# A three-stage decoder layer on one core: other orders, PSUM banks and waits in the third stage

## The chip, the core and the metric

The kernel runs on one core of a Trainium2 chip. The core's engines are TensorE (PE in the profile; its weight loads are a row of their own, PEld), VectorE (DVE), ScalarE (ACT), GpSimd (POOL) and SyncE (SP, which only issues transfers). Each works through its own instructions in order; they meet through semaphores. The metric is the device time of one execution in microseconds (us), as the median of several.

## The reference, cut to what matters

`x` is 64 sequences of 64 tokens, 128 wide. A self attention and a cross attention come first. The third part, which is where the change lies, is six layers of local attention and a gated feed-forward, each on the shifted residual:

```python
for i in range(DEPTH):                      # 6
    x = attn_layer(shift_tokens(x), Wqkv[i], q_scale[i], k_scale[i], Wo[i]) + x
    x = ffn_layer(shift_tokens(x), ln_g[i], ln_b[i], W1[i], b1[i], W2[i], b2[i]) + x

# attn_layer, 16 heads of 64:
q, k, v = heads(x @ Wqkv)
q = l2norm(q) * qs;  k = l2norm(k) * ksc
q = q * cos * scale + rotate_half(q) * sin * scale
k = k * cos * inv + rotate_half(k) * sin * inv
out = softmax(8 * q k^T, masked) v
return out @ Wo

# ffn_layer, inner width 341:
a, gate = split(layernorm(x) * g + bln) @ W1 + b1
return a * gelu(gate) @ W2 + b2
```

## The kernel before

A tile is two sequences, 128 tokens, so a layer has 32 tiles and the third stage (the function `local`) has N = 192 of them. It is one software pipeline: every engine runs a loop over `i`, and each body names the steps of an iteration with the tile that each works on, for instance `queries(i, 0)` beside `scores(i - 1)`, `head_outputs(i - 4)` and `ff_in(i - 7)`. In a full iteration TensorE thus does one of each step, for tiles of different age. Nothing schedules this: the order in an engine's loop is the order in which it works, and the waits are written by hand.

The steps, by their lines in the profile, in TensorE's order before: the turned input (L1008, `bank<-ident,ystat`), the output projection (L1160), the four products that make queries and keys (L1032), the turning of queries and keys (L1008, `bank<-ident,R`), the second feed-forward product (L1024), the turning of the probabilities (L1008, `bank<-ident,P`) and of the normalised input (L1008, `bank<-ident,xn`), the **value products** `head_outputs` (probabilities times values, L1144, 32 products of 64x64), the **scores** (mask L1098, then L1103, 32 products of 64x64), the **values** (L1083, 4 products of 512 columns), and the first feed-forward product (L1128). A float32 product is two MATMUL records and two LDWEIGHTS records in the trace, so 32 products read as x64.

ScalarE copies each result out of PSUM (L1194: `xcT`, `qT`, `kT`, `PT`, `OT`, `V`), squares queries and keys (L1219), and takes exponents (L1232) and gates (L1259). VectorE makes the rotation (L1319), the sums of squares (L1332), maxima, row sums and the gated product. GpSimd issues two accumulating transfers per tile, `queries_added` (L1419) and `keys_added` (L1424), which add the rotated half to the other in place in `R`; it refines the inverse lengths in twelve small operations (L1465 to L1472), scales keys (L1432) and scores (L1438), and makes the probability products (`probs_scaled`, L1444, `P<-P,inv_sum`).

PSUM has eight banks and every step uses a fixed one. A bank that two steps share makes the later wait for whoever reads the earlier result; most waits at the head of TensorE's steps are of that kind. A `Counted` semaphore counts several parts per tile, and its list says in which order they come, so a changed order changes these lists too.

## Time and profile before

| | |
|---|---|
| time, median of 3 runs | 3522.41 us (3520.82 to 3523.2) |
| time of the profiled execution | 3525.89 us, its span 3524.1 us |
| TensorE clock granted, mean | 0.993 of full speed |
| TensorE matmul busy | 3377.9 us, 96% of the span |
| VectorE, ScalarE, GpSimd busy | 80%, 79%, 70% |
| third stage, first input turned | at 569.4 us, the last at 3446.0 us |

The span runs from the first to the last instruction. Busy time is when an instruction of that engine is recorded; a float32 product's second record overlaps the first, and a record's end is modelled, so that a busy share of 96% is not a measure of what is lost between products. In the chain of work the pieces follow each other without overlap; in the timeline they overlap.

### The profile page before, as it was taken

Reading aid. Unit: us, or ns where it says so; the run is one execution under the profiler, and the core shown is the slowest. Engines: PE = TensorE matmul, PEld = TensorE weight load, DVE = VectorE, ACT = ScalarE, POOL = GpSimd, SP = SyncE. Lnnn points to the kernel's source line nnn. Section 1 sums busy time; section 2 is a strip of 40 time slices with the busy share of each in tenths; the row PEclk is TensorE's granted clock in tenths of the full one; section 3 lists DMA queues with packets and bytes.
Section 4 is the critical chain, followed back from the end, with each engine's and each line's share of the span. In section 5 each row is a group of like instructions: output and inputs, shape, how many; then the busy total and the mean of one; then the engine's idle time right before and its main releaser. Section 6 shows DMA issues by size and latency. Waiting matters only on the chain.

```text
span 3524.1 us, 120975 instructions
## 1 busy us (share of the span) xinstructions
PE 3377.9 (96%) x49605; PEld 2495.3 (71%) x49605; DVE 2811.5 (80%) x5297; ACT 2792.7 (79%) x5522; POOL 2475.5 (70%) x4812
## 2 busy tenths in 40 slices
PE   8989997999999999999999999999999999999997
PEld 5778774677777777777777777777777777777776
DVE  6834445888888888888888888888888888888885
ACT  5756664688888888888888888888888888888885
POOL 5622224777777777777777777777777777777774
PEclk9999998999999999999999999999999999999999
DMA  3000002444444444444444444444444444444441
GB/s 101 3 10 8 9 6 50 92 82 82 82 81 89 95 82 82 80 88 97 82 82 82 83 90 93 82 82 80 90 96 83 82 82 88 78 85 83 88 85 39
DMA packets 200382, 260.17 MB, mean 74 GB/s; under 512 B 123161, under 2 KB 145438, under 8 KB 199838
## 3 DMA queue, kind: packets, MB, share of 16 engines
q0 software_dynamic: 55296, 201.35, 30.4%
q1 hardware_dynamic: 143820, 50.88, 5.8%
q8 instruction: 400, 6.55, 0.8%
q14 instruction: 144, 1.18, 0.1%
q10 hardware_dynamic: 722, 0.21, 0.0%
HBM read 23.95 MB, written 2.10 MB: 7 GB/s over the span
## 4 chain that ended last, share of the span: by engine, by line
PE 78%; issue 2%; DVE 1%; POOL 1%; DMA 1%; ACT 0%; SPq 0%; POOLq 0%; DVEq 0%
PE bank L1032 18%; PE bank L1008 16%; PE bank L1083 10%; PE bank L1160 10%; PE bank L1128 7%; PE bank L1144 6%; PE bank L1103 5%; PE bank L1024 3%; PE bank L1098 2%; DVE R L1319 1%; DMA R<-R 1%; POOL R L1432 0%; POOL P L1444 0%; DVE ss L1332 0%; POOL P L1438 0%
## 5 line engine op out<-in xcount | busy, mean ns | idle before, releaser
L1319 DVE TENSOR_TENSOR R<-bank,tables 128x1024 f32<-128x1024 f32 x768 | 903.6, 1218 | 167.5 <-ACT sq L1219 127.4
L1032 PE MATMUL bank<-WA,xcT 128*128 128x512 f32 x1536 | 757.6, 596 | 1.8 <-ACT xcT L1194 1.8
L1008 PEld LDWEIGHTS bank<-ident,R 128*128 128x128 f32 x3072 | 371.6, 141 | 307.0 <-issue 299.9
L1444 POOL TENSOR_TENSOR P<-P,inv_sum 128x512 f32<-128x512 f32 x384 | 458.2, 1193 | 13.1 <-DVE inv_sum L1373 12.1
L1332 DVE TENSOR_REDUCE ss<-sq 128x16 f32<-128x1024 f32 x384 | 460.3, 1199 | 0.0
L1219 ACT ACTIVATE sq<-bank 128x512 f32<-128x512 f32 x768 | 438.2, 595 | 23.9 <-PE bank L1032 23.5
L1432 POOL TENSOR_TENSOR R<-R,rn 128x512 f32<-128x512 f32 x384 | 392.3, 1042 | 88.1 <-DMA R<-R 73.4
L1008 PE MATMUL bank<-ident,R 128*128 128x128 f32 x3072 | 429.8, 273 | 3.3 <-POOL R L1432 2.4
L1438 POOL TENSOR_TENSOR P<-P,rn 128x512 f32<-128x512 f32 x384 | 402.5, 1048 | 2.1 <-DVE P L1361 2.1
L1160 PE MATMUL bank<-WO,OT 128*128 128x128 f32 x3072 | 386.4, 279 | 1.7 <-ACT OT L1194 1.7
L1083 PE MATMUL bank<-WV,xcT 128*64 128x512 f32 x1536 | 376.0, 606 | 3.2 <-DVE R L1319 2.9
L1160 PEld LDWEIGHTS bank<-WO,OT 128*128 128x128 f32 x3072 | 357.4, 192 | 5.3 <-ACT OT L1194 1.9
L1194 ACT ACTIVATE PT<-bank 128x512 f32<-128x512 f32 x384 | 230.2, 599 | 146.8 <-PE bank L1008 146.8
L1194 ACT ACTIVATE kT<-bank 128x512 f32<-128x512 f32 x384 | 233.3, 608 | 133.6 <-PE bank L1008 133.6
L1032 PEld LDWEIGHTS bank<-WA,xcT 128*128 128x128 f32 x1536 | 248.6, 192 | 97.2 <-issue 94.3
L1128 PE MATMUL bank<-xnT,W 128*128 128x128 f32 (+1 forms) x2304 | 287.5, 275 | 0.0
L1194 ACT ACTIVATE V<-bank 128x512 f32<-128x512 f32 x384 | 230.5, 600 | 71.9 <-PE bank L1083 71.9
L1008 PEld LDWEIGHTS bank<-ident,P 128*128 128x128 f32 x1536 | 170.8, 141 | 164.1 <-issue 155.1
L1103 PE MATMUL bank<-kT,qT 64*64 64x64 f32 x12288 | 234.5, 219 | 54.6 <-issue 54.6
L1103 PEld LDWEIGHTS bank<-kT,qT 64*64 64x64 f32 x12288 | 229.7, 135 | 71.0 <-issue 61.9
L1361 DVE TENSOR_TENSOR P<-bank,mx 128x512 f32<-128x512 f32 x384 | 263.2, 686 | 6.7
L1128 PEld LDWEIGHTS bank<-xnT,W 128*128 128x128 f32 (+1 forms) x2304 | 264.8, 180 | 0.1
(154 smaller groups left out, 7082.5 us busy)
## 6 DMA issues: line engine op xcount, KB each, us to landing
R<-R POOLq DMA_DIRECT2D x384, 512.0 KB, 5.3
WA<-in_wqkv SPq DMA_DIRECT2D x24, 256.0 KB, 2.8
ystat<-Y SPq DMA_DIRECT2D x192, 32.0 KB
ystat<-Y SPq DMA_DIRECT2D x384, 15.8 KB
ys<-Y SPq DMA_DIRECT2D x192, 32.0 KB
ys<-Y SPq DMA_DIRECT2D x384, 15.8 KB
WV<-in_wqkv SPq DMA_DIRECT2D x6, 512.0 KB, 5.9
WO<-in_wo SPq DMA_DIRECT2D x6, 512.0 KB, 4.3
```

The lines of the kernel that those rows point to most:

```text
L1008: return nc.tensor.transpose(dst, src, m.ident[:, :])
L1032: mm(b[QK_BANK[n, half]][:, :], m.xsT[:, t % 2, :], cols[:, half, :, :], start=True, stop=True)\
L1083: last = mm(V_BANK[bb][64 * e:64 * e + 64, :], m.xsT[:, t % 2, bb * 64:bb * 64 + 64], cols[:, e, :, :], start=True, stop=True)
L1103: last = mm(S_BANK[a][64 * bb:64 * bb + 64, hp * 64:(hp + 1) * 64], m.qT[head, t % 2, at:at + 64], m.kT[head, t % 2, at:at + 64], start=Fa ...
L1128: last = mm(FF_BANK[c][0:rows, side * 128:(side + 1) * 128], m.W1[:, off + at:off + at + rows], m.xnT[:, t % 2, :], start=True, stop=True)
L1160: last = mm(OUT[:, 0:128], m.OT[:, t % 2, at:at + 128], wo[:, c * 128:(c + 1) * 128], start=(c == 0), stop=(c == PAIRS - 1))
L1194: return nc.scalar.activation(dst, src, ACT.Copy)
L1219: nc.scalar.activation(by_half[:, half, :, :], b[QK_BANK[n, half]][:, :].rearrange("p (h d) -> p h d", d=32), ACT.Square)\
L1319: tt(both, src.unsqueeze(1).to_broadcast([128, 2, 16, 32]), tab.unsqueeze(2).to_broadcast([128, 2, 16, 32]), ALU.mult).then_inc(s.rotated. ...
L1332: nc.vector.tensor_reduce(m.ss[:, t % 2, 16 * n:16 * n + 16], m.sq[:, n, :].rearrange("p (h d) -> p h d", d=HD), AX.X, ALU.add)\
L1438: tt(part, part, wide(m.rn[:, t % 4, a:16:2]), ALU.mult).then_inc(s.scaled.sem, 1)
L1444: tt(part, part, wide(m.inv_sum[:, t % 2, 8 * a:8 * a + 8]), ALU.mult).then_inc(s.normal.sem, 1)
```

## The change

It writes the loops of TensorE, ScalarE, VectorE and GpSimd in the third stage in another order, gives every step other PSUM banks, and writes the waits that the new sharing needs. No instruction is added or removed: there are as many products, copies, reductions and transfers, of the same shapes. GpSimd's `probs_scaled(i - 2, 1)` at an iteration's end becomes `probs_scaled(i - 3, 1)` behind the next one's `queries_added`, and `inverse_deviation` moves from the end of one iteration to behind `keys_added` of the next. The core of the diff:

```diff
-    QK_BANK = {(QUERIES, 0): 3, (QUERIES, 1): 6, (KEYS, 0): 1, (KEYS, 1): 2}
-    TURNED_IN, TURNED_OUT = b[4], b[6]
-    KT_BANK, QT_BANK, V_BANK = (b[7], b[0]), (b[7], b[4]), (b[1], b[4])
-    S_BANK, PT_BANK, PV_BANK = (b[5], b[6]), (b[0], b[0]), (b[4], b[3])
-    OUT, FF_BANK, FF_OUT = b[0], (b[2], b[1], b[7]), b[5]
+    QK_BANK = {(QUERIES, 0): 6, (QUERIES, 1): 5, (KEYS, 0): 7, (KEYS, 1): 1}
+    TURNED_IN, TURNED_OUT = b[6], b[5]
+    KT_BANK, QT_BANK, V_BANK = (b[2], b[4]), (b[0], b[3]), (b[2], b[5])
+    S_BANK, PT_BANK, PV_BANK = (b[0], b[7]), (b[6], b[5]), (b[4], b[6])
+    OUT, FF_BANK, FF_OUT = b[4], (b[2], b[1], b[3]), b[3]
...
             def input_turned(t):
                 if exists(t):
                     pe.wait_ge(s.ystat[t % 2], 48 * (t // 2) + 48)
-                    at_least(pe, s.v_copied.sem, s.v_copied.upto(1, t))
+                    at_least(pe, s.p_copied.sem, s.p_copied.upto(0, t - 3))
                     turned(TURNED_IN[:, 0:128], m.ystat[:, t % 2, :]).then_inc(s.x_turned, 1)
...
             def keys_turned(t, j):
                 if exists(t):
                     pe.wait_ge(s.k_scaled.sem, s.k_scaled.upto(j, t + 1))
-                    if j == 0:
-                        pe.wait_ge(s.q_copied.sem, s.q_copied.upto(0, t + 1))
-                    elif t < 8:
-                        at_least(pe, s.y1, t - 3)
                     for n in range(4):
                         at = j * 512 + n * 128
                         last = turned(KT_BANK[j][:, n * 128:(n + 1) * 128], m.R[:, KEYS, 0, at:at + 128])
...
             def values(t, bb):
                 if exists(t):
                     cols = m.WV[:, :].rearrange("p (j e n) -> p e j n", e=2, n=128)
-                    if bb == 0:
-                        pe.wait_ge(s.rotated.sem, s.rotated.upto((KEYS, 0), t + 1))
+                    if bb == 1:
                         pe.wait_ge(m.w_v, 16 * layer(t) + 16)
+                        at_least(pe, s.xn_copied, t - 5)
+                        if t < 7:
+                            pe.wait_ge(s.rotated.sem, s.rotated.upto((QUERIES, 1), t + 1))
                     else:
-                        at_least(pe, s.o_copied.sem, s.o_copied.upto(0, t - 3))
+                        at_least(pe, s.k_copied.sem, s.k_copied.upto(0, t))
                     for e in range(2):
...
             def scores(t):
                 if exists(t):
-                    pe.wait_ge(s.q_copied.sem, s.q_copied.upto(1, t + 1))
+                    pe.wait_ge(s.q_copied.sem, s.q_copied.upto(0, t + 1))
                     pe.wait_ge(s.k_copied.sem, s.k_copied.upto(0, t + 1))
-                    at_least(pe, s.xn_copied, t - 4)
-                    at_least(pe, s.y, t - 6)
-                    if t < 6:
-                        pe.wait_ge(s.rotated.sem, s.rotated.upto((QUERIES, 1), t + 2))
+                    pe.wait_ge(s.rotated.sem, s.rotated.upto((KEYS, 0), min(t + 2, N)))
+                    if t == N - 1:
+                        pe.wait_ge(s.less.sem, s.less.upto(1, t))
...
                     pe.wait_ge(s.v_copied.sem, s.v_copied.upto(0, min(t + 8, N)))
-                    pe.wait_ge(s.rotated.sem, s.rotated.upto((KEYS, 1), min(t + 8, N)))
+                    at_least(pe, s.y, t)
+                    if t == 0:
+                        pe.wait_ge(s.rotated.sem, s.rotated.upto((KEYS, 1), 8))
...
                 input_turned(i)
                 out_projection(i - 5)
                 queries(i, 0)
-                queries_turned(i - 1, 1)
                 queries(i, 1)
                 queries_turned(i - 1, 0)
+                queries_turned(i - 1, 1)
                 keys(i, 0)
                 keys(i, 1)
                 keys_turned(i - 1, 1)
+                ff_out(i - 8)
                 keys_turned(i - 1, 0)
-                ff_out(i - 8)
-                probs_turned(i - 3, 1)
                 normal_turned(i - 6)
                 head_outputs(i - 4)
+                values(i, 1)
+                values(i, 0)
                 scores(i - 1)
-                values(i, 0)
-                values(i, 1)
+                probs_turned(i - 3, 1)
                 probs_turned(i - 3, 0)
                 ff_in(i - 7)
...
                 gates(i - 8)
                 squares(i, QUERIES, 0)
                 squares(i, QUERIES, 1)
+                queries_out(i - 1, 1)
                 queries_out(i - 1, 0)
+                keys_out(i - 1, 1)
+                squares(i, KEYS, 1)
+                normal_out(i - 6)
                 squares(i, KEYS, 0)
-                keys_out(i - 1, 1)
-                queries_out(i - 1, 1)
-                squares(i, KEYS, 1)
                 keys_out(i - 1, 0)
-                normal_out(i - 6)
+                values_out(i, 1)
+                exponents(i - 2, 1)
+                outputs_out(i - 4, 1)
+                outputs_out(i - 4, 0)
+                values_out(i, 0)
+                probs_out(i - 3, 1)
+                probs_out(i - 3, 0)
                 exponents(i - 2, 0)
-                outputs_out(i - 4, 0)
-                probs_out(i - 3, 1)
-                exponents(i - 2, 1)
                 normalised(i - 5)
-                outputs_out(i - 4, 1)
-                values_out(i, 0)
-                probs_out(i - 3, 0)
-                values_out(i, 1)
...
                 squares_summed(i, QUERIES)
-                ff_added(i - 8)
                 rotary(i, KEYS, 0)
                 rotary(i, KEYS, 1)
                 squares_summed(i, KEYS)
+                ff_added(i - 8)
                 seeded(i)
                 maximum(i - 1, 0)
-                maximum(i - 1, 1)
-                less_maximum(i - 1, 1)
                 row_sums(i - 2, 0)
                 less_maximum(i - 1, 0)
+                row_sums(i - 2, 1)
+                maximum(i - 1, 1)
+                attention_added(i - 4)
+                inverse_sums(i - 2, 1)
+                gated(i - 7)
+                less_maximum(i - 1, 1)
                 inverse_sums(i - 2, 0)
-                attention_added(i - 4)
-                gated(i - 7)
-                row_sums(i - 2, 1)
-                inverse_sums(i - 2, 1)
...
                 queries_added(i)
+                probs_scaled(i - 3, 1)
                 probs_scaled(i - 3, 0)
                 keys_added(i)
+                inverse_deviation(i - 5)
                 inverse_lengths(i)
+                keys_scaled(i, 1)
+                scores_scaled(i - 1, 0)
                 keys_scaled(i, 0)
-                keys_scaled(i, 1)
                 scores_scaled(i - 1, 1)
-                probs_scaled(i - 2, 1)
-                scores_scaled(i - 1, 0)
-                inverse_deviation(i - 4)
```

What stands in TensorE's row in the middle of a full iteration, before, from the second feed-forward product (L1024) to the first (L1128). `P` are the probabilities, `xn` the normalised input, `PT,V` the value products, `kT,qT` the scores, `WV,xcT` the values:

```order
L1024 MATMUL bank<-W,H 128x128 x3
L1008 MATMUL bank<-ident,P 128x128 x4
L1008 MATMUL bank<-ident,xn 128x128
L1144 MATMUL bank<-PT,V 64x64 x32
L1098 MATMUL bank<-causalb,identb 64x512 x4
L1103 MATMUL bank<-kT,qT 64x64 x32
L1083 MATMUL bank<-WV,xcT 64x512 x4
L1008 MATMUL bank<-ident,P 128x128 x4
L1128 MATMUL bank<-xnT,W 128x128 x4
```

The same piece of TensorE's row in the change:

```order
L1008 MATMUL bank<-ident,R 128x128 x4
L1025 MATMUL bank<-W,H 128x128 x3
L1008 MATMUL bank<-ident,R 128x128 x4
L1008 MATMUL bank<-ident,xn 128x128
L1146 MATMUL bank<-PT,V 64x64 x32
L1082 MATMUL bank<-WV,xcT 64x512 x4
L1096 MATMUL bank<-causalb,identb 64x512 x4
L1101 MATMUL bank<-kT,qT 64x64 x32
L1008 MATMUL bank<-ident,P 128x128 x8
L1130 MATMUL bank<-xnT,W 128x128 x4
```

Value products and scores stood side by side with only the mask's four products between them; now the four products of the values stand between the two. Both turnings of the probabilities stand behind the scores, where one stood ahead of the value products.

ScalarE's row before, from the exponents (`P<-P`) of an iteration's middle to the turned input's copy (`xcT`) of the next:

```order
L1194 ACTIVATE OT<-bank 128x512
L1194 ACTIVATE PT<-bank 128x512
L1232 ACTIVATE P<-P 128x512
L1242 ACTIVATE xn<-ys,nmr,rstd 128x128
L1194 ACTIVATE OT<-bank 128x512
L1194 ACTIVATE V<-bank 128x512
L1194 ACTIVATE PT<-bank 128x512
L1194 ACTIVATE V<-bank 128x512
L1194 ACTIVATE xcT<-bank 128x128
L1259 ACT_TABLE_LOAD
L1259 ACTIVATE G<-bank,b1col 128x128 x2
```

ScalarE's row in the change, from the copies of queries to the second exponents:

```order
L1193 ACTIVATE qT<-bank 128x512 x2
L1193 ACTIVATE kT<-bank 128x512
L1218 ACTIVATE sq<-bank 128x16x32
L1208 ACTIVATE xnT<-bank,bcol,gcol 128x128
L1218 ACTIVATE sq<-bank 128x16x32
L1193 ACTIVATE kT<-bank 128x512
L1193 ACTIVATE V<-bank 128x512
L1231 ACTIVATE P<-P 128x512
L1193 ACTIVATE OT<-bank 128x512 x2
L1193 ACTIVATE V<-bank 128x512
L1193 ACTIVATE PT<-bank 128x512 x2
L1231 ACTIVATE P<-P 128x512
```

The first copy of values (`V<-bank`) now stands ahead of exponents and outputs, and between the two copies of values stand one exponent and both copies of outputs. The fourth squares (`sq`) stand behind the copy of the normalised input.

GpSimd's row before, from the scaled keys (`R<-R,rn`) to the second accumulating transfer (`DMA R<-R`):

```order
L1432 TENSOR_TENSOR R<-R,rn 128x512 x2
L1438 TENSOR_TENSOR P<-P,rn 128x512
L1444 TENSOR_TENSOR P<-P,inv_sum 128x512
L1438 TENSOR_TENSOR P<-P,rn 128x512
L1450 TENSOR_SCALAR vare<-mv 128x1
L1452 TENSOR_TENSOR rstd<-vare,minus_half 128x1
L1454 TENSOR_SCALAR nmr<-mv,rstd 128x1
L1419 DMA R<-R 128x1024
L1444 TENSOR_TENSOR P<-P,inv_sum 128x512
L1424 DMA R<-R 128x1024
```

GpSimd's row in the change, from the first scaled keys to the inverse deviation:

```order
L1431 TENSOR_TENSOR R<-R,rn 128x512
L1437 TENSOR_TENSOR P<-P,rn 128x512
L1431 TENSOR_TENSOR R<-R,rn 128x512
L1437 TENSOR_TENSOR P<-P,rn 128x512
L1418 DMA R<-R 128x1024
L1443 TENSOR_TENSOR P<-P,inv_sum 128x512 x2
L1423 DMA R<-R 128x1024
L1449 TENSOR_SCALAR vare<-mv 128x1
L1451 TENSOR_TENSOR rstd<-vare,minus_half 128x1
L1453 TENSOR_SCALAR nmr<-mv,rstd 128x1
```

Both probability products (`P<-P,inv_sum`) stand between the two transfers' issues, where one stood, and the three small operations of the inverse deviation stand behind the second issue, ahead of the inverse lengths.

## Rows read from the trace of the kernel before

**Rows 1.** The page: busy time, share of the span and instructions of each engine

```profile
PE 3377.9 (96%) x49605; PEld 2495.3 (71%) x49605; DVE 2811.5 (80%) x5297; ACT 2792.7 (79%) x5522; POOL 2475.5 (70%) x4812
```

**Rows 2.** Tile `ystat`, 710 to 3447 us: duration min/median/max ns, first and last start us

```profile
L1008 PE MATMUL bank<-ident,ystat x182: 299/299/303, 710.0 to 3446.0; 128*128 128x128 f32 x182
```

**Rows 3.** The chain, an iteration without a stop: start us, us, what

```profile
1060.30 1.85 PE bank L1160 x16
...
1064.31 0.44 PE bank L1008 x4
...
1068.55 1.09 PE bank L1144 x64
1069.64 0.36 PE bank L1098 x4
1070.01 0.93 PE bank L1103 x64
1070.94 1.87 PE bank L1083 x8
1072.81 0.59 PE bank L1008 x4
1073.39 1.33 PE bank L1128 x12
...
1074.96 1.85 PE bank L1160 x16
```

**Rows 4.** The chain, the scores of two iterations with a stop

```profile
1053.98 0.69 PE bank L1103 x47
1054.67 1.14 issue
1055.82 0.47 PE bank L1103 x17
...
2143.26 0.31 PE bank L1103 x19
2143.57 1.05 issue
```

**Rows 5.** Waits, 710 to 3447 us, TensorE: us in total, times, longest

```profile
PE bank L1103 <- issue: 53.7, 59, 1.5
```

**Rows 6.** Transfer queues (packets, MB, share of 16 engines): whole span, then 1053.0 to 1053.4 us

```profile
q8 instruction: 400, 6.55, 0.8%
...
q8 instruction: 1, 0.02, 20.2%
```

**Rows 7.** Timeline: start us, us, engine, what, idle before and whom for

```profile
1070.71 0.65 ACT L1232 ACTIVATE P<-P 128x512 f32<-128x512 f32 x1
...
1071.61 0.61 ACT L1194 ACTIVATE OT<-bank 128x512 f32<-128x512 f32 x1
1072.09 0.62 ACT L1194 ACTIVATE V<-bank 128x512 f32<-128x512 f32 x1
...
2009.27 1.94 PE L1083 MATMUL bank<-WV,xcT 128*64 128x512 f32 x8
...
2010.39 0.60 ACT L1194 ACTIVATE V<-bank 128x512 f32<-128x512 f32 x1 [0.80 <-PE bank L1083]
```

**Rows 8.** Timeline, GpSimd and TensorE in the iteration of rows 3

```profile
1061.72 2.04 POOL L1432 TENSOR_TENSOR R<-R,rn 128x512 f32<-128x512 f32 x2 [0.98 <-DMA R<-R]
...
1066.30 1.04 PE L1008 MATMUL bank<-ident,R 128*128 128x128 f32 x8
...
1067.71 0.23 POOL L1450 TENSOR_SCALAR vare<-mv 128x1 f32<-128x1 f32 x1 [0.93 <-DVE mv L1327]
...
1068.90 0.94 POOL L1419 DMA_DIRECT2D R<-R  x1
...
1071.49 0.88 POOL L1424 DMA_DIRECT2D R<-R  x1 [0.56 <-DVE R L1319]
1073.05 0.23 POOL L1465 TENSOR_TENSOR rn_a<-seed 128x32 f32<-128x32 f32 x1 [0.69 <-DVE seed L1344]
```

More of the change, by code:

```diff
@@ L913, in local @@
     s.x_turned, s.x_copied = sem("local_x_turned"), sem("local_x_copied")
-    s.qk, s.squared, s.rotated = counted("qk", *four), counted("squared", *four), counted("rotated", *four)
+    s.qk, s.squared, s.rotated = counted("qk", *four), counted("squared", (QUERIES, 0), (QUERIES, 1), (KEYS, 1), (KEYS, 0)), counted("rotated", *four)
     s.summed, s.seed, s.lengths = counted("summed", QUERIES, KEYS), sem("local_seed"), sem("local_lengths")
-    s.q_added, s.k_added, s.k_scaled = sem("local_q_added"), sem("local_k_added"), counted("k_scaled", 0, 1)
+    s.q_added, s.k_added, s.k_scaled = sem("local_q_added"), sem("local_k_added"), counted("k_scaled", 1, 0)
     s.k_turned, s.k_copied = counted("k_turned", 1, 0), counted("k_copied", 1, 0)
-    s.q_turned, s.q_copied = counted("q_turned", 1, 0), counted("q_copied", 0, 1)
-    s.v, s.v_copied = counted("v", 0, 1), counted("v_copied", 0, 1)
-    s.scores, s.mx, s.less = sem("local_scores"), counted("mx", 0, 1), counted("less", 1, 0)
-    s.scaled, s.probs, s.row_sum = counted("scaled", 1, 0), counted("probs", 0, 1), counted("row_sum", 0, 1)
-    s.inverse, s.normal = counted("inverse", 0, 1), counted("normal", 1, 0)
+    s.q_turned, s.q_copied = counted("q_turned", 0, 1), counted("q_copied", 1, 0)
+    s.v, s.v_copied = counted("v", 1, 0), counted("v_copied", 1, 0)
+    s.scores, s.mx, s.less = sem("local_scores"), counted("mx", 0, 1), counted("less", 0, 1)
+    s.scaled, s.probs, s.row_sum = counted("scaled", 0, 1), counted("probs", 1, 0), counted("row_sum", 0, 1)
+    s.inverse, s.normal = counted("inverse", 1, 0), counted("normal", 1, 0)
     s.p_turned, s.p_copied = counted("p_turned", 1, 0), counted("p_copied", 1, 0)
-    s.o, s.o_copied, s.wo, s.y1 = sem("local_o"), counted("o_copied", 0, 1), sem("local_wo"), sem("local_y1")
+    s.o, s.o_copied, s.wo, s.y1 = sem("local_o"), counted("o_copied", 1, 0), sem("local_wo"), sem("local_y1")
     s.stats, s.var, s.vare, s.pow, s.rstd = (sem("local_stats"), sem("local_var"), sem("local_vare"), sem("local_pow"),
@@ L981, in weights @@
                     if 2 <= n < 6:
-                        at_least(sp, s.v.sem, s.v.upto(1, first))
+                        at_least(sp, s.v.sem, s.v.upto(0, first))
                         load_input_weights(sp, m, l + 1, (l + 1) % 2, n - 2)
@@ L990, in weights @@
                     if n == TILES - 1:
-                        sp.wait_ge(s.v.sem, s.v.upto(1, first + TILES))
+                        sp.wait_ge(s.v.sem, s.v.upto(0, first + TILES))
                         load_value_weights(sp, m, l + 1)
@@ L1039, in queries @@
                         pe.wait_ge(m.w_in, 64 * layer(t) + 64)
-                    else:
-                        at_least(pe, s.less.sem, s.less.upto(1, t - 1))
                     heads_in(t, QUERIES, half)
@@ L1045, in keys @@
                 if exists(t):
-                    if half == 1 and t < 2:
-                        at_least(pe, s.rotated.sem, s.rotated.upto((KEYS, 1), t))
+                    if half == 0:
+                        at_least(pe, s.less.sem, s.less.upto(1, t - 1))
+                    if t < 2:
+                        at_least(pe, s.rotated.sem, s.rotated.upto((KEYS, half), t))
                     heads_in(t, KEYS, half)
@@ L1065, in queries_turned @@
                     if j == 0:
+                        at_least(pe, s.less.sem, s.less.upto(0, t))
+                    else:
                         at_least(pe, s.h, 3 * (t - 6))
-                    elif t == N - 1:
-                        pe.wait_ge(s.v_copied.sem, s.v_copied.upto(1, t + 1))
                     for n in range(4):
@@ L1111, in probs_turned @@
                     if j == 0:
-                        pe.wait_ge(s.p_copied.sem, s.p_copied.upto(1, t + 1))
+                        at_least(pe, s.o_copied.sem, s.o_copied.upto(1, t))
                     else:
-                        pe.wait_ge(s.k_copied.sem, s.k_copied.upto(1, min(t + 3, N)))
+                        pe.wait_ge(s.v_copied.sem, s.v_copied.upto(1, min(t + 4, N)))
+                        if t >= N - 3:
+                            pe.wait_ge(s.xn_copied, t - 2)
                     for n in range(4):
@@ L1215, in squares @@
                     act.wait_ge(s.qk.sem, s.qk.upto((n, half), t + 1))
-                    if half == 0:
+                    if (n, half) in ((QUERIES, 0), (KEYS, 1)):
                         at_least(act, s.summed.sem, s.summed.upto(n, t))
@@ L1311, in rotary @@
                         if n == QUERIES:
-                            at_least(dve, s.q_turned.sem, s.q_turned.upto(0, t))
-                        elif t < 9:
+                            at_least(dve, s.q_turned.sem, s.q_turned.upto(1, t))
+                        elif t < 7:
                             at_least(dve, s.k_turned.sem, s.k_turned.upto(0, t))
@@ L1427, in keys_scaled @@
                 if exists(t):
-                    if j == 0:
+                    if j == 1:
                         pool.wait_ge(s.k_added, 16 * t + 16)
```

8 lines of the change are left out of this document (3 added, 5 removed).

## Prediction

> **What bounds the kernel now.** I read the page first: TensorE is busy for 96% of the span, the next engine for 80% [rows 1]. So the question is at what pace TensorE's row runs, and what interrupts it. For the pace I took the 182 turned inputs from the tenth iteration on: they start at 710.0 and, the last, at 3446.0 us, so 181 periods of 15.12 us [rows 2]. Then I followed the chain of work through single iterations. In the undisturbed one every piece is TensorE's and each begins where the one before ends; from output projection to output projection it takes 1074.96 - 1060.30 = 14.66 us [rows 3]. So the average iteration loses 15.12 - 14.66 = 0.46 us, over 181 of them 82.5 us. That is what a change without fewer instructions can win.
>
> The chain says where: in the scores. Undisturbed, their 64 records take 0.93 us [rows 3]. In other iterations the chain has 47 of them, then 1.14 us of "issue", then 17; or 19, then 1.05 us, then the rest [rows 4]. A wait for data would stand ahead of a step's first product, never behind the 47th or the 19th. The list of waits has 59 such stops in these 181 iterations, 53.7 us idle, the longest 1.5 us [rows 5]. Idle time is counted from the modelled end of the last product, so it understates: the first of the two shown makes the scores 0.69 + 1.14 + 0.47 = 2.30 us, 1.37 longer than undisturbed for 1.14 shown. With 0.23 us more for each of the 59, they cost 67 us of the 82.5. The next largest wait of a TensorE product in that stretch is under 2 us in total, so I put most of the remaining 15 us down to stops too short to show behind a modelled end.
>
> What is late is code. The queue of kind "instruction" moves 400 packets, 6.55 MB, 16.4 KB each [rows 6]; TensorE has 2 x 49605 records [rows 1], 248 to a packet. A packet begins within 1053.0 to 1053.4 us and takes 0.202 x 16 x 0.4 = 1.29 us [rows 6], so it lands between 1054.3 and 1054.7; the scores go on at 1055.82 [rows 4]. From its start to the resumption are 2.4 to 2.8 us. Value products, mask and scores are 128 + 8 + 128 = 264 records, more than a packet holds, and run through in 1.09 + 0.36 + 0.93 = 2.38 us [rows 3]; the other steps run at 0.11 us a product or slower [rows 3]. So only there can TensorE use up a portion before the next is in, and only where a portion ends in the scores does it show.
>
> **The change, part by part.** Nothing is added or removed, so the sum has only waits and joints.
>
> *Values between value products and scores.* The four value steps take 1.87 us [rows 3] and issue only 16 records. Where the portion was asked for during the value products, they put 1.87 us ahead of the same record of the scores; the longest stop was 1.5 us idle, some 1.7 lost [rows 5, 4]. So the stops that are due to this pair vanish. The bounds: nothing vanishes (0), or all that iterations lose (82.5 us). A portion that runs out behind the scores instead meets the turnings and the feed-forward product, which take 0.11 us a product [rows 3] and so leave time. I take 82.5 less 2 for some short stops that stay: **-80 us**.
>
> *Joints between steps of different shape.* Four turnings take 0.44 us behind a product of their own width and 0.59 us behind the values [rows 3], so a joint can cost 0.15 us. The values now stand between two steps in quarters of the array, and the probabilities' turnings leave the values' side. One joint more or fewer is at most 0.15 x 191 = 29 us either way; counting both orders, one is gained where one is lost, and I take 0.
>
> *ScalarE's copy of values, for which the first feed-forward product waits.* Its bank is now shared with the second half of the values. A copy starts 1.12 us after the values start [rows 7]. Behind it stand one exponent and two copies of outputs, a copy each 0.48 us after the last, the exponent at most 0.65, the copy itself 0.62 [rows 7]: 1.12 + 0.48 + 0.65 + 0.48 + 0.48 + 0.62 = 3.83 us after the values' start. TensorE arrives at the feed-forward product after 1.87 + 0.36 + 0.93 + 8 x 0.11 = 4.04 us. It is hidden by the scores and the turnings, with 0.2 us to spare; gone, each 0.1 us costs 19 us.
>
> *GpSimd: both probability products between the issues, the deviation behind the second.* Before, the second issue comes 2.59 us after the first and has idled 0.56 us for VectorE's rotation [rows 8]. The remaining 2.03 us are the issue, 0.94, and one product, 1.09. With two products it is 3.12 us, 0.5 too long, if the first issue stayed put. It doesn't: the deviation, 1.19 us from 1067.71 to 1068.90 [rows 8], and one product no longer stand ahead of it. Behind the second issue the deviation's 1.19 us now delays the inverse lengths, which used to idle 0.69 us for VectorE [rows 8]: at most 0.5 us later. The scaled keys start 1.42 us into the iteration (1061.72 - 1060.30), the first half is done 1.0 later, and TensorE wants it at 1066.30, 6.0 us in: 3.5 us of cover [rows 8]. Cost 0. The keys' rotation, whose squares now stand behind two more ScalarE steps of half a microsecond, comes out of the same cover.
>
> *VectorE* is busy for 80% [rows 1]; its maxima and row sums change places with 2.9 us an iteration to spare. Cost 0.
>
> Sum against the profiled execution: span 3524.1 - 80 = 3444 us. The median of the runs shown, 3522.4, is 1.7 lower: **3442 us**.
>
> **The rivals.**
>
> *Some stops stay.* GpSimd's first transfer is issued up to 2 us earlier, over the value products, and its packets then share the engines with the code's. If that makes portions late by half a microsecond more, the stops near the scores' end stay: a third of them, 27 us, gives 3469. For it: the packet's own time varies. Against: 1.87 us of cover for a mean loss of 67 / 59 = 1.1 us a stop.
>
> *A small new wait each iteration.* The 0.2 us at the feed-forward product are the thinnest cover I found. If ScalarE is 0.4 us later than laid out, TensorE waits 0.2 us, 191 x 0.2 = 38 us: 3480.
>
> *It doesn't do what I say.* The stops go to another place in the row, or have another cause: 3522. The Trainium skill, "Runtime: NRT & Kernel Launch", section "Instruction fetch mechanics", speaks for that: TensorE holds 2048 instructions and crossing a block is mostly hidden. By that rule the order of steps could not matter, and the time stays at 3522. The trace speaks against it: stops at changing places inside a step, and a packet that lands 1.1 to 1.5 us before the scores go on [rows 4, 6].
>
> *Slower.* GpSimd is one row, and the keys for TensorE stand behind two rotations, a transfer, twelve small operations and a product. If VectorE's keys come so late that this chain uses up its 3.5 us of cover, TensorE waits in every iteration; it decides from 3.5 + 0.46 = 4.0 us of lateness on. At 4.2 us the period is 14.66 + 0.7 = 15.36, and 191 x 0.24 = 46 us make 3568. I count at most 0.5 us from GpSimd and 1 us from ScalarE, so this needs a wait that I have not seen.
>
> **How the numbers follow.** Likeliest, 65 in 100: the stops go, 3442 us; its own range, from the joints and the uncounted 15 us, is 3426 to 3458. Some stops stay 13, a new small wait 9, no effect 8, slower 5. The range 3426 to 3482 holds the likeliest case in most of its spread and the next two for the most part, together about 8 in 10. A measurement of this kernel can tell about 0.2%, 7 us, from no change: faster 0.87, within it 0.07, slower 0.06.
>
> **What would show it right or wrong.** Right: the waits of TensorE on "issue" in the scores fall from 53.7 us to under 5, the mean period from 15.12 to 14.7, and 400 instruction packets stay. Wrong: "issue" at another line with a like sum; TensorE waiting for `V` at L1130, or for the scaled keys at L1008, some 190 times; a free iteration that is not 14.66 but 14.8 (joints).

## The result, and the profile after

The changed kernel takes 3399.44 us (median of 4, 3397.73 to 3402.21) against 3522.80 (3520.82 to 3524.92): a ratio of 0.965, with a 95% interval of 0.9634 to 0.9667, or 123 us less. The forecast was 3442, 80 us less; the measured time lies outside its range of 3426 to 3482, on the fast side.

The page after, engines and the queue of code [rows 1, 6], and the turned inputs from the tenth iteration on [rows 2]:

```profile
PE 3315.8 (98%) x49605; PEld 2471.6 (73%) x49605; DVE 2767.3 (81%) x5297; ACT 2803.6 (82%) x5522; POOL 2481.0 (73%) x4812
...
q8 instruction: 399, 6.54, 0.8%
```

```profile
L1008 PE MATMUL bank<-ident,ystat x182: 272/273/273, 704.6 to 3322.2; 128*128 128x128 f32 x182
```

Instructions and code are as many. The period is (3322.2 - 704.6) / 181 = 14.46 us, where it was 15.12 and 14.7 was forecast. One more number has changed without being looked for: the same turning is recorded with 273 ns instead of 299. The chain after, one iteration, to be held against [rows 3]:

```profile
1066.26 1.79 PE bank L1159 x16
...
1072.80 0.67 PE bank L1025 x6
1073.47 0.55 PE bank L1008 x5
1074.02 1.09 PE bank L1146 x64
1075.11 1.87 PE bank L1082 x8
1076.98 0.34 PE bank L1096 x4
1077.32 0.93 PE bank L1101 x64
1078.25 1.02 PE bank L1008 x8
1079.27 1.33 PE bank L1130 x12
1080.60 0.11 PE bank L1008
1080.71 1.34 PE bank L1159 x12
```

From output projection to output projection 1080.71 - 1066.26 = 14.45 us, 0.21 less than the undisturbed iteration of before. Value products, scores, values and the feed-forward product read the same. What is shorter is the output projection, 1.79 for 1.85, and what lies between the last feed-forward product and it. The list of waits, 710 to 3300 us, has no wait of a TensorE product at all in this kernel. GpSimd waits there (us in total, times, longest) for VectorE before the second issue, and hardly for a transfer:

```profile
POOL R L1423 <- DVE R L1318: 200.3, 173, 1.2
...
POOL R L1431 <- DMA R<-R: 3.5, 6, 1.1
```

To divide the gain I took, for 176 iterations of each trace, the time from the first product of a step to the first of the next. This counts what a modelled end hides. Means in ns:

| step | before | after | difference |
|---|---|---|---|
| scores | 1454 | 1036 | -418 |
| first feed-forward product | 1430 | 1331 | -99 |
| output projection | 1850 | 1787 | -63 |
| turned input | 153 | 109 | -44 |
| value products | 1128 | 1092 | -36 |
| values | 1884 | 1867 | -17 |
| mask | 215 | 240 | +25 |
| the others | | | 0 within 7 each |

The sum is -652 ns an iteration, by 191 periods -125 us. There are two parts. In scores, value products and values the time above each step's median was 70.0 + 2.9 + 2.9 us over the 176 iterations and is 0.6 now: 0.43 us an iteration, 82 in all. These are the stops, but for some 1.6 us of waits of the values for VectorE. The three lines from the feed-forward product to the output projection give 0.206 us an iteration, 39 in all. No view marks them as idle. The rest, 0.02 us, I put down to joints.

### The profile page after: what moved, and what is told of

It reads as the page before. It is cut to its first block, busy times and chain, and to the rows that moved or that the text cites. A ratio compares the mean times of both kernels' runs of the same rounds, so it can differ in the third digit from the quotient of the medians.

```text
span 3398.5 us, 120772 instructions
## 1 busy us (share of the span) xinstructions
PE 3315.8 (98%) x49605; PEld 2471.6 (73%) x49605; DVE 2767.3 (81%) x5297; ACT 2803.6 (82%) x5522; POOL 2481.0 (73%) x4812
## 4 chain that ended last, share of the span: by engine, by line
PE 80%; DMA 1%; POOL 1%; DVE 1%; ACT 0%; issue 0%; SPq 0%; POOLq 0%; DVEq 0%
PE bank L1033 19%; PE bank L1008 17%; PE bank L1082 10%; PE bank L1159 10%; PE bank L1130 8%; PE bank L1146 6%; PE bank L1101 5%; PE bank L1025 4%; PE bank L1096 2%; DMA R<-R 1%; DMA ys<-Y 0%; DVE R L1318 0%; POOL R L1431 0%; POOL P L1437 0%; ACT PT L1193 0%
## 5 line engine op out<-in xcount | busy, mean ns | idle before, releaser
L1033 PE MATMUL bank<-WA,xcT 128*128 128x512 f32 x1536 | 726.5, 596 | 3.0 <-ACT xcT L1193 2.1
L1443 POOL TENSOR_TENSOR P<-P,inv_sum 128x512 f32<-128x512 f32 x384 | 447.2, 1329 | 2.9 <-DVE inv_sum L1372 2.9
L1218 ACT ACTIVATE sq<-bank 128x512 f32<-128x512 f32 x768 | 431.3, 587 | 18.9 <-PE bank L1033 18.9
L1431 POOL TENSOR_TENSOR R<-R,rn 128x512 f32<-128x512 f32 x384 | 400.5, 1043 | 35.2 <-DMA R<-R 5.7
L1033 PEld LDWEIGHTS bank<-WA,xcT 128*128 128x128 f32 x1536 | 263.3, 191 | 190.5 <-issue 185.7
L1159 PE MATMUL bank<-WO,OT 128*128 128x128 f32 x3072 | 374.6, 275 | 0.0
L1366 DVE TENSOR_REDUCE row_sum<-P 128x8 f32<-128x512 f32 x384 | 261.6, 682 | 124.3 <-ACT P L1231 124.3
L1423 POOL DMA_DIRECT2D R<-R x192 | 167.4, 872 | 231.0 <-DVE R L1318 217.7
L1130 PE MATMUL bank<-xnT,W 128*128 128x128 f32 (+1 forms) x2304 | 289.2, 276 | 5.5 <-DVE Y L1299 5.5
L1130 PEld LDWEIGHTS bank<-xnT,W 128*128 128x128 f32 (+1 forms) x2304 | 265.5, 180 | 6.9 <-issue 6.8
L1352 DVE TENSOR_REDUCE mx<-bank 128x8 f32<-128x512 f32 x384 | 262.4, 683 | 2.5 <-PE bank L1101 2.5
L860 POOL TENSOR_TENSOR P<-P,inv_sum 128x512 f32<-128x512 f32 x64 | 65.5, 1042 | 246.5 <-DVE inv_sum L832 246.5
```

Of the source, the lines that this page charges most:

```text
L1033: mm(b[QK_BANK[n, half]][:, :], m.xsT[:, t % 2, :], cols[:, half, :, :], start=True, stop=True)\
L1130: last = mm(FF_BANK[c][0:rows, side * 128:(side + 1) * 128], m.W1[:, off + at:off + at + rows], m.xnT[:, t % 2, :], start=True, stop=True)
L1159: last = mm(OUT[:, 0:128], m.OT[:, t % 2, at:at + 128], wo[:, c * 128:(c + 1) * 128], start=(c == 0), stop=(c == PAIRS - 1))
L1218: nc.scalar.activation(by_half[:, half, :, :], b[QK_BANK[n, half]][:, :].rearrange("p (h d) -> p h d", d=32), ACT.Square)\
L1431: tt(part, part, wide(m.rn[:, t % 4, 16 + 8 * j:24 + 8 * j]), ALU.mult).then_inc(s.k_scaled.sem, 1)
L1443: tt(part, part, wide(m.inv_sum[:, t % 2, 8 * a:8 * a + 8]), ALU.mult).then_inc(s.normal.sem, 1)
```

## The experiments

The question was whether the two parts are what I took them for, and what the new order of GpSimd has to do with it.

**Two products that nobody reads, in two places.** Added to the kernel before: two products of 512 columns, once between value products and mask, once ahead of the queries.

```diff
+            def dead(t, bank):
...
+                    for half in range(2):
+                        mm(b[bank][:, :], m.xsT[:, t % 2, :], cols[:, half, :, :], start=True, stop=True)
...
                 head_outputs(i - 4)
+                dead(i, 7)
                 scores(i - 1)
```

> The kernel before, with two more products of 512 columns per iteration (queries' input times key weights, four records of 0.43 us, result never read) between value products and scores. They cost 192 x 1.72 = 330 us of TensorE's time. Theory (late instructions): they do what the moved values do, the stops in the scores vanish and give back 70 to 80 us, so 3522 + 330 - 75 = about 3777 us, and TensorE waits less than 5 us for 'issue' in the scores. Rival (the stops have another cause, the gain came from banks and orders): 3522 + 330 = 3852 us, with some 54 us of 'issue' as before.

> The kernel before, with the same two unread products, but behind the output projection and ahead of the queries, so that value products and scores stay side by side. Theory (late instructions): the stops stay, 50 to 60 of them, and the time is about 3522 + 330 = 3852 us. Rival (any longer iteration gives the other engines time and so removes the stops): the stops go here too, about 3777 us.

Between the two steps: 3804.33 us (3799.43 to 3809.81), ratio 1.08 (1.0779 to 1.0821). Ahead of the queries: 3860.89 us (3854.65 to 3864.24), 1.0957 (1.0939 to 1.0974). The first in the timeline (start us, us, engine, what):

```profile
1063.06 1.16 PE L1144 MATMUL bank<-PT,V 64*64 64x64 f32 x64
1064.15 1.98 PE L1175 MATMUL bank<-WA,xcT 128*128 128x512 f32 x4
1066.07 0.41 PE L1098 MATMUL bank<-causalb,identb 64*64 64x512 bf16 x4
```

and the waits of the second, 710 to 3600 us:

```profile
PE bank L1103 <- issue: 51.6, 63, 1.4
```

The pair costs 1.92 us between the steps (1066.07 - 1064.15), 1.72 elsewhere. So 192 of them are 368 us in the first kernel, which with 3523.5 makes 3891; it is 87 faster than that, and has no stop left. The second is 3523.5 + 330 = 3854 and 7 more, with all stops. Only the place differs (and with it the bank that the pair writes): time between value products and scores takes the stops away, and by this sum 87 us are their whole price, where the division above gave 82. The first kernel is 27 us above what I had expected: the pair costs 38 us more in that place, and the stops gave back 12 more. So two full-width products between two steps in quarters of the array cost 0.2 us more than among steps of full width.

**Only the turned input's bank.** In the chain of before the output projection begins 1074.96 - 1073.39 = 1.57 us after the feed-forward product, 1.44 in the chain after. TURNED_IN shared bank 4 with the second half of the values. I gave it bank 3 in the kernel before, whose readers are long done, wrote out the waits that other steps had through the old one, and left the orders alone.

```diff
-    TURNED_IN, TURNED_OUT = b[4], b[6]
+    TURNED_IN, TURNED_OUT = b[3], b[6]
...
-                    at_least(pe, s.v_copied.sem, s.v_copied.upto(1, t))
+                    at_least(pe, s.o_copied.sem, s.o_copied.upto(1, t - 4))
...
```

> The kernel before, with the turned input in bank 3 instead of bank 4, so that it no longer waits for the copy of the second half of the values; the waits that others had through that one are written out. Nothing else moves. Theory (a wait hidden beneath modelled ends, 0.19 us in every iteration: last feed-forward product to turned input 0.21 instead of 0.11 us, turned input to output projection 0.14 instead of 0.11, output projection 1.85 instead of 1.79): 0.19 x 191 = 36 us less, about 3486 us, and the stops in the scores stay. Rival (the faster pieces of the changed kernel come from smoother delivery of instructions or from other banks of the products): no difference, 3522 us.

3485.91 us (3478.83 to 3490.1), ratio 0.9892 (0.9875 to 0.991): 38 us less. The timeline of before, and of this kernel:

```profile
1073.23 1.49 PE L1128 MATMUL bank<-xnT,W 128*128 128x128 f32 x12
...
1073.92 0.59 ACT L1194 ACTIVATE V<-bank 128x512 f32<-128x512 f32 x1
...
1074.66 0.30 PE L1008 MATMUL bank<-ident,ystat 128*128 128x128 f32 x1
...
1074.80 0.67 PE L1160 MATMUL bank<-WO,OT 128*128 128x128 f32 x4
```

```profile
1038.99 1.49 PE L1130 MATMUL bank<-xnT,W 128*128 128x128 f32 x12
1040.32 0.27 PE L1008 MATMUL bank<-ident,ystat 128*128 128x128 f32 x1
1040.43 1.95 PE L1161 MATMUL bank<-WO,OT 128*128 128x128 f32 x16
1042.22 1.02 PE L1034 MATMUL bank<-WA,xcT 128*128 128x512 f32 x2
```

Before, the copy of values ends at 1073.92 + 0.59 = 1074.51, and the turned input starts 0.15 later, 1.43 us after the feed-forward product. With the other bank it is 1.33 us, the turning is followed after 0.11 instead of 0.14, and the output projection takes 1.79 instead of 1.85. Nothing in the full iterations of before marks this as idle: the feed-forward product is recorded until 1074.72, past the start of the turning that waited. The row of weight loads has the trace of it: in before the turned input's load starts 0.03 us ahead of its product (1074.63), in the changed kernel 0.11 us ahead, while the products before it still run. The stops stayed, as the waits of this kernel show (710 to 3300 us):

```profile
PE bank L1105 <- issue: 49.9, 57, 1.3
```

**The changed kernel with such a wait put back.** The turned input waits in addition for `s.probs`, ScalarE's last exponents of the iteration before, which end a little late for it.

```diff
             def input_turned(t):
...
+                    at_least(pe, s.probs.sem, s.probs.upto(0, t - 2))
```

> The changed kernel, in which the turned input waits in addition for ScalarE's last exponents of the iteration before, which by the layout end at about the same time as the copy of values did in the kernel before. Theory (hidden wait): the iteration gets some 0.1 to 0.25 us longer, 20 to 45 us more than the changed kernel's 3399, with next to no idle time shown for it. Rival (the pieces are faster for another reason): no difference, 3399 us.

3450.82 us (3449.94 to 3453.66), ratio to before 0.9796: 51 us more than the changed kernel, where I had expected 20 to 45. Its timeline, then its chain:

```profile
1076.43 0.63 ACT L1232 ACTIVATE P<-P 128x512 f32<-128x512 f32 x1
...
1077.21 0.30 PE L1008 MATMUL bank<-ident,ystat 128*128 128x128 f32 x1
```

```profile
1075.86 1.33 PE bank L1131 x12
1077.19 0.02 issue
1077.21 0.30 PE bank L1008
1077.51 1.92 PE bank L1160 x16
```

The exponents end at 1076.43 + 0.63 = 1077.06, and the turned input starts 0.15 us later, as it did behind the copy of values in before. Output projection follows feed-forward product after 1077.51 - 1075.86 = 1.65 us instead of 1.44, and then takes 1.92 instead of 1.79, in an iteration that is 0.08 us longer than the median one. By medians it is 0.18 us in the feed-forward step, 0.03 in the turning, 0.06 in the projection: 0.27 us, by 191 52 us. The chain shows 0.02 of it as a gap. The wait is longer than that of before, hence more than 39 us.

**Only the values moved.** The kernel before with the values between value products and scores, and the wait that this needs.

```diff
+                        at_least(pe, s.q_copied.sem, s.q_copied.upto(1, t))
...
                 head_outputs(i - 4)
-                scores(i - 1)
                 values(i, 0)
                 values(i, 1)
+                scores(i - 1)
```

> The kernel before, with its four value steps moved between value products and scores and nothing else moved; banks as before, one wait written out that was implied by the scores' wait. Theory: the stops in the scores go (-80 us) and the hidden wait of the turned input stays, but the first values share bank 1 with the keys, whose rotation on VectorE ends about 0.5 us after the value products do; TensorE waits for it in every iteration, 190 x 0.5 = 95 us, shown as a wait of L1083 for VectorE's L1319. Sum 3522 - 80 + 95 = about 3537 us. Rival (the new order alone is the gain, the banks are beside the point): 3442 us.

3550.77 us (3547.7 to 3562.16), ratio 1.0081 (1.0055 to 1.0107): slower. The stops are gone, and in their place (710 to 3480 us):

```profile
PE bank L1084 <- DVE R L1320: 89.9, 177, 1.2
```

The first half of the values writes a bank that VectorE's rotation of the keys reads, and now comes 1.3 us sooner, in every iteration: the step ahead is 1627 ns for 1092, 0.5 us by 191 = 102 us lost for some 80 won. The move pays only with other banks.

**Both edits.** The move and the bank together in the kernel before.

> Two of the edits to the kernel before, together: the values stand between value products and scores, and the turned input is in another bank, so that it waits for no copy of values. If the two gains are independent, the result is that of the move alone, 3551, less the 37 us of the bank alone: 3514, with the feed-forward product at 1330 ns and the turned input at 109 ns. If the wait for VectorE's rotation, which the move alone met, takes up what the bank gives (TensorE is then held by VectorE and not by its own row), it stays at 3545 to 3555.

3523.38 us (3520.37 to 3524.44), ratio 0.9987 (0.9977 to 0.9997) to the 3529.21 of the runs beside it, that is 33 us less than the move alone by the ratios. The bank gives 33 of its 38 us; the step that waits for the rotation grew from 1627 to 1670 ns. The gains add up, nearly. What still separates this kernel from the changed one is the wait for the rotation, which the change's banks do not have.

**Something shorter between.** The kernel before with the turning of one half of the probabilities between value products and scores, 0.44 us of work.

```diff
-                probs_turned(i - 3, 1)
                 normal_turned(i - 6)
                 head_outputs(i - 4)
+                probs_turned(i - 3, 1)
                 scores(i - 1)
```

> The kernel before, with the four turnings of the probabilities' second half moved from ahead of the value products to between them and the scores: 0.44 us and a joint instead of 1.87 us of cover. Theory (late instructions): stops of 0.4 to 1.6 us each get 0.5 to 0.6 us shorter, so 'issue' in the scores falls from 54 to 20 to 35 us; the additional joint between wide and quarter steps costs 0.1 to 0.2 us an iteration, 20 to 38 us, and the time is 3510 to 3540 us. Rival (the stops do not depend on what stands there): 54 us of 'issue' and 3542 to 3560 us.

3555.39 us (3548.83 to 3558.94), ratio 1.0086. Waits, 710 to 3447 us:

```profile
PE bank L1103 <- issue: 34.1, 52, 1.3
```

Half a microsecond of cover shortens the stops from 70 to 50 us start to start and removes few of them; the idle time falls as I had expected, to 20 to 35 us. The time doesn't: it is above my 3510 to 3540 and in the range of the rival. What the place costs is more than the cover gives: the turnings take 586 for 439 ns, a joint, and the normalised input 323 for 202. Together 0.27 us an iteration or 51 us: 3523 - 20 + 51 = 3554. The second of the two is again a hidden wait, as the timeline shows:

```profile
1073.96 0.59 ACT L1194 ACTIVATE qT<-bank 128x512 f32<-128x512 f32 x1
...
1074.70 1.16 PE L1144 MATMUL bank<-PT,V 64*64 64x64 f32 x64
```

The value products write bank 4, where the turned queries were, and are made to wait for ScalarE's copy of these. It ends at 1074.55, 0.15 us ahead of them, and so it does in every iteration (0.144 to 0.146); in before it is at least 0.46 us ahead. They come 0.44 us sooner here.

**Twice the value products in the changed kernel.** Each is computed twice, so that 256 records stand in the step.

```diff
-                    for j in range(4):
+                    for again, j in [(0, 0), (0, 1), (0, 2), (0, 3), (1, 0), (1, 1), (1, 2), (1, 3)]:
...
```

> The changed kernel, which computes the value products twice in a row, the second time over the same results: 128 more records of weights and products, 0.94 us, per iteration. Theory (late instructions): 256 records in a row use up a portion as value products and scores did, so besides 192 x 0.94 = 181 us of work the stops come back, 40 to 80 us of 'issue', now in the value products (L1146) or behind them: 3620 to 3660 us. Rival (the stops belong to the scores' data or banks and are gone): 3399 + 181 = 3580 us, no 'issue'.

3760.25 us (3752.07 to 3768.5), ratio 1.0662. Waits, 710 to 3500 us:

```profile
PE bank L1146 <- issue: 64.1, 50, 1.8
PE bank L1101 <- issue: 49.8, 40, 1.8
```

The stops are back, nearly all at two lines. The second set takes 0.93 us, 179 in all; the stops take 173 us start to start: 3399 + 179 + 173 = 3751. I had expected one set of stops and 3620 to 3660 us. My reading of the second set, which no run tests, is that the values' 1.87 us cover only part of the next portion when the one before was late already.

**GpSimd's order of before in the changed kernel.** Both moved lines back at the iteration's end.

```diff
                 queries_added(i)
-                probs_scaled(i - 3, 1)
                 probs_scaled(i - 3, 0)
                 keys_added(i)
-                inverse_deviation(i - 5)
...
+                probs_scaled(i - 2, 1)
+                inverse_deviation(i - 4)
```

> The changed kernel, with GpSimd's probability products and inverse deviation where they stood before: one product at the end of an iteration, one between the issues of the transfers, the deviation last. Theory (TensorE's row bounds all of it, GpSimd has cover): no difference from the changed kernel, 3399 us within 7. Rival (the products between the issues are part of the gain): over 15 us slower than the changed kernel.

3475.65 us (3472.51 to 3478.01), ratio 0.9862: 76 us slower than the changed kernel, where I expected no difference. Waits, 710 to 3400 us:

```profile
POOL R L1431 <- DMA R<-R: 275.5, 181, 4.1
...
PE bank L1008 <- POOL R L1431: 39.1, 75, 1.5
```

GpSimd waits for the keys' transfer in every iteration, 1.5 us on average, where the changed kernel has 3.5 us in all. Its timeline, then that of the changed kernel:

```profile
1502.57 0.94 POOL L1418 DMA_DIRECT2D R<-R  x1
1503.25 1.35 POOL L1443 TENSOR_TENSOR P<-P,inv_sum 128x512 f32<-128x512 f32 x1
1504.25 1.21 POOL L1423 DMA_DIRECT2D R<-R  x1
...
1512.91 1.04 POOL L1431 TENSOR_TENSOR R<-R,rn 128x512 f32<-128x512 f32 x1 [3.62 <-DMA R<-R]
```

```profile
1507.38 0.95 POOL L1418 DMA_DIRECT2D R<-R  x1
1508.08 2.33 POOL L1443 TENSOR_TENSOR P<-P,inv_sum 128x512 f32<-128x512 f32 x2
1511.62 0.88 POOL L1423 DMA_DIRECT2D R<-R  x1 [1.21 <-DVE R L1318]
```

The issues are 1.68 us apart instead of 4.24. Two transfers of 512 KB then run over each other, and the second is late. To see which line does it, I put each back by itself, `probs_scaled` and then `inverse_deviation`.

> The changed kernel with one line moved back on GpSimd: the probability product of the older half stands at an iteration's end again, and not between the issues of the two accumulating transfers; the inverse deviation stays behind the second issue. The spacing theory: the product between the issues (1.09 us) is what keeps the two transfers apart; without it they are issued some 3 us apart instead of 4.2, the keys' transfer takes between 4.4 and 6.5 us, and TensorE waits for scaled keys in a part of the iterations: 3410 to 3460. The rival, that the deviation's place is what cost the 76 us of the run with the whole old order: no difference here, 3399 to 3406.

> The changed kernel with both probability products between the issues, and only the inverse deviation's three small operations back at the iteration's end, ahead of the first issue. The spacing theory: the issues stay over 3 us apart, nothing of the transfers changes, 3397 to 3410. The rival, that the deviation ahead of the first issue (1.2 us with its wait for VectorE) makes the queries' transfer late and pushes it against the keys': TensorE waits for scaled keys, 3440 to 3480.

With the product back 3405.69 us (3403.55 to 3408.31), ratio 0.9654 (0.9639 to 0.9668); with the deviation back 3413.27 us (3412.3 to 3417.11), 0.9677 (0.9662 to 0.9691), both to 3529.21. The first is the changed kernel's ratio; the second is 0.3% above it, and 7 us of that lie behind the last turned input (84 us to the end instead of 76). So neither line alone carries the 76 us. The first lies below what I had expected and in its rival's range; the second is 3 us above what I had expected and far below its rival. What goes with the length of the keys' transfer is the distance of the two issues. Medians of 175 iterations, from the issue of the keys' transfer to the end of its last packet:

| kernel | issues apart, us | keys' transfer, us | over 6 us |
|---|---|---|---|
| the change | 4.24 | 4.36 | 3 times |
| product back | 3.32 | 4.75 | 5 |
| deviation back | 2.84 | 5.22 | 5 |
| before | 2.59 | 5.15 | 13 |
| both back | 1.67 | 6.49 | 115 |

Either line alone keeps them at least 2.8 us apart, and the keys in time. Only without both is the transfer later than TensorE's cover in most iterations. No run changes the distance alone: with both back the keys' issue itself also comes later, 12.2 us after the turned input instead of 11.7 by the medians, and this half a microsecond can be part of the 76 us.

**The product's move in the kernel before.** There both probability products stand between the issues, and TensorE's order as it was.

```diff
                 queries_added(i)
+                probs_scaled(i - 3, 1)
                 probs_scaled(i - 3, 0)
...
-                probs_scaled(i - 2, 1)
```

> The kernel before with one line moved on GpSimd: the older half's probability product stands between the two issues, next to the other one, as in the change. TensorE turns those probabilities early in this kernel, ahead of the value products. If the orders of the engines have to fit each other, TensorE waits for GpSimd in every iteration, by my layout some 2 to 3 us: 3800 to 4100. If GpSimd has the spare time that its 70% suggest, and the spacing of the transfers is a gain of its own: 3500 to 3530.

4507.55 us (4485.32 to 4524.54), ratio 1.2773. TensorE's and GpSimd's timeline:

```profile
2012.58 0.83 PE L1024 MATMUL bank<-W,H 128*128 128x128 f32 x6
2016.40 1.11 PE L1008 MATMUL bank<-ident,P 128*128 128x128 f32 x4 [2.98 <-POOL P L1444]
...
2017.66 1.99 PE L1144 MATMUL bank<-PT,V 64*64 64x64 f32 x64
```

```profile
2013.12 0.23 POOL L1450 TENSOR_SCALAR vare<-mv 128x1 f32<-128x1 f32 x1 [6.44 <-DVE mv L1327]
...
2014.32 0.94 POOL L1419 DMA_DIRECT2D R<-R  x1
2015.00 2.34 POOL L1444 TENSOR_TENSOR P<-P,inv_sum 128x512 f32<-128x512 f32 x2
```

TensorE needs the probabilities ahead of the value products. They now stand behind the deviation, which waits 6.44 us for VectorE. TensorE waits 3 us in every iteration, and after the wait its clock is lower. Windows (us, TensorE busy, granted clock, share and GB/s of the transfers):

```profile
2005.40:2012.50 7.10, 7.09 (x41) 1.00 0.10 23
2016.40:2021.60 5.20, 5.20 (x137) 0.50 0.94 176
```

Before the wait TensorE has its full clock, 2.4 GHz, and after it half, 1.2: turnings, value products and scores take 0.91, 1.76 and 1.86 us for 0.44, 1.11 and 1.06. Of the 5.7 us by which the median period grows, 3.1 are the wait and 2.6 the clock, both by the steps' times from first product to first product. I had expected 3800 to 4100 with the wait alone. GpSimd's spare 30% do not help when its row stands in another order than TensorE wants.

## Why the prediction was off, by its steps

**"What is late is code", and the stops vanish: right, in place and size.** Forecast -80, measured 82 us by the trace and 87 in the kernel with two unread products between the steps. No TensorE product waits on "issue" in the scores any more, and the code is 399 packets. That it depends on how many records run in how short a time is shown three times: cover of 1.9 us removes the stops, 0.5 us shortens them, twice the records bring them back. One detail was coarse. With those of its sequencer TensorE has 102,539 records, which makes 256 to a packet and not 248; and counted so, the 59 longest stops in before all stand ahead of record 193 or 194 of a block of 256. TensorE goes on 2.2 to 2.8 us after the start of the packet that came last, some 1.4 us after its end. The rival by the Trainium skill's "Runtime: NRT & Kernel Launch", "Instruction fetch mechanics", that crossing is mostly hidden and the order cannot matter, gave 3522; the runs with equal products in two places, 57 us apart, decide against it.

**"In the undisturbed one every piece ... begins where the one before ends; ... 14.66 us": the step that failed.** I took the iteration without a stop for the pace of TensorE's row, and called the 0.46 us above it the whole that a change could win. But that iteration, like every other, contained a wait of 0.2 us, of the turned input on ScalarE's copy of values in the same bank. The pieces follow each other in the chain because a product's end is modelled, and a wait shorter than that tail does not show. The bank alone gave 38 us, a like wait in the changed kernel took 51. The trace of before had it: copy ends at 1074.51, turning starts at 1074.66. And in the first iterations of the stage, from 560 to 710 us, which I had left out, the wait stands bare in the list of waits of before (us in total, times, longest):

```profile
PE bank L1008 <- ACT V L1194: 7.4, 7, 1.3
```

I read the diff's new `TURNED_IN` as one bank among eight and costed it at nothing.

**Joints, 0: right for the whole, by cancelling.** 0.02 us an iteration are left over. By itself a joint cost 0.2 us with the unread products, more than the 0.15 that I took as the bound, and 0.15 with the turnings between. The 0.15 itself was misread: I took it from the chain's pieces, which begin at a modelled end; from first product to first product the two turnings take 0.44 and 0.49 us, a joint of 0.05.

**ScalarE's copy of values and the feed-forward product: right.** No wait at L1130, nor a hidden one: the copy ends 0.37 us ahead of the product, 0.2 more than behind the hidden waits, which is what I had forecast to spare.

**GpSimd, 0: right for this change, and for a reason that I hadn't.** I costed how much later the second issue would be, and found cover. What the new order does is to hold the transfers apart; the other orders of the change need that, 76 us of it. **VectorE, 0**: no wait for it appears at TensorE in the change, but 0.5 us an iteration if the values are moved without their new banks.

Of the rivals, stops that stay, a new small wait and slower keys did not come; the last is the form in which the change fails with GpSimd's old order, though by overlap of transfers and not by a long chain. The range reached to the rivals on the slow side and 16 us on the fast one: the missing case was a wait already there.

## What to carry to other kernels

An iteration without idle time in the chain is not yet the free pace: take the time from first product to first product of each step, and look for steps of one shape that take longer in one place than in another; there check the semaphore of the shared bank. A copy that ends 0.144 us ahead of such a step in every iteration is a second sign, but not enough by itself: in the changed kernel the mask starts 0.145 us after a copy of values for which it doesn't wait. Where many small products run side by side, part them with a step of few long ones, and give it banks that are free at its new place. And an order on one engine is worth what the others' orders make of it: of four edits tried alone, one gained, two lost and one cost 28%.

## What the runs showed of the hardware that I had not expected

- The hidden wait of before stands in the records in three pieces: 100 ns ahead of the turned input, 27 behind it, and 61 in the output projection, between its first record and its second (173 ns for 112, the other 14 distances as without the wait). All kernels with the wait have the third piece and none without has it; why the delay is divided so stays open.
- The second of two accumulating transfers of 512 KB each takes 4.4 us when issued 4.2 us after the first, and 6.5 when issued 1.7 after; the first takes 4.6 in that case and is not slowed. These are medians, and the distance was never changed alone.
- Steps in quarters of the array take another time by what stands beside them, by medians: value products, mask and scores in a row take 1112, 215 and 1056 ns, with a full-width step between them 1092, 240 and 1032.
- A wait of 3 us in every iteration is followed by 5 us at half the clock, nearly doubling its cost.
